# One instruction per row for the hidden layer, and the weighted sums in two bursts

## What is computed

```python
hi = jnp.einsum('bsh,hk->bsk', x, W1[:H])
hj = jnp.einsum('bsh,hk->bsk', x, W1[H:])
h = jax.nn.relu(hi[:, :, None, :] + hj[:, None, :, :] + b1)
y = jnp.einsum('bijk,kl->bijl', h, W2) + b2
y = _layernorm(y, gamma, beta)
out = jnp.einsum('bij,bijh->bih', adj, y)
```

## Time and profile before

| | |
|---|---|
| median of 3 runs | 2622.48 us |
| the profiled execution, first to last instruction | 2621.4 us |
| granted TensorE clock, mean | 0.998 |
| TensorE busy (weight loads) | 2577.0 us, 98% (2049.5 us, 78%) |
| VectorE busy | 2337.8 us, 89% |
| ScalarE busy | 2332.6 us, 89% |
| GpSimd busy | 1999.1 us, 76% |

### The profile page before, as it was taken

How to read it: one execution, slowest core, us unless ns; L and a number is a source line. 1 busy time by engine, 2 the same in 40 slices (tenths; PEclk the granted TensorE clock), 3 DMA queues, 4 the chain that set the end, 5 groups by cost and what they waited for, 6 DMA issues and landing times.

```text
span 2621.4 us, 77145 instructions
## 1 busy us (share of the span) xinstructions
PE 2577.0 (98%) x21263; PEld 2049.5 (78%) x21263; DVE 2337.8 (89%) x18135; ACT 2332.6 (89%) x3650; POOL 1999.1 (76%) x1163
## 2 busy tenths in 40 slices
PE   8999999999999999999999999999999999999997
PEld 7777777777777777777777777777777777777774
DVE  7889988989899889998898989988988999989897
ACT  7899899899998998989989889999899898998996
POOL 7777777777777777777777777777777777777773
PEclk9999999999999999999999999999999999999999
DMA  0000000000000000000000000000000000000000
GB/s 17 8 12 7 11 7 10 11 6 11 11 6 11 6 11 11 6 11 11 6 11 6 11 11 6 11 10 7 11 6 11 11 6 11 8 8 11 6 7 7
DMA packets 48051, 23.49 MB, mean 9 GB/s; under 512 B 6208, under 2 KB 47808, under 8 KB 47808
## 3 DMA queue, kind: packets, MB, share of 16 engines
q1 hardware_dynamic: 46512, 21.12, 2.9%
q10 hardware_dynamic: 1296, 0.20, 0.0%
HBM read 17.11 MB, written 4.19 MB: 8 GB/s over the span
## 4 chain that ended last, share of the span: by engine, by line
PE 58%; DVE 24%; issue 11%; ACT 6%; POOL 0%; ACTq 0%; DVEq 0%; DMA 0%
PE y_ps L529 42%; DVE squares L517 16%; PE agg_ps L573 12%; DVE q L517 3%; ACT y L263 3%; DVE x1e L488 2%; ACT h L281 1%; ACT L334 1%; PE prep_ps L529 1%; PE tail_ps L529 1%; DVE o_sb L455 1%; PE tail_ps L584 1%; PE att_ps L529 1%; DVE eT L509 0%; DVE si_cols L499 0%
## 5 line engine op out<-in xcount | busy, mean ns | idle before, releaser
L252 POOL TENSOR_TENSOR h<-bT,aT 128x1024 f32<-128x1024 f32 x1024 | 1951.1, 1919 | 584.3 <-PE y_ps L529 572.9
L529 PEld LDWEIGHTS y_ps<-w_pair,h 128*128 128x128 f32 x16384 | 1885.7, 192 | 313.0 <-DVE q L517 260.3
L529 PE MATMUL y_ps<-w_pair,h 128*128 128x128 f32 x16384 | 1991.3, 278 | 21.9 <-DVE q L517 9.3
L517 DVE CUSTOM_DVE_ANT_0 squares<-y_ps,y 128x128 bf16<-128x128 f32 x8192 | 1842.3, 282 | 185.0 <-ACT y L263 171.2
L263 ACT ACTIVATE y<-y_ps 128x508 f32<-128x508 f32 x2048 | 1162.4, 595 | 190.8 <-PE y_ps L529 173.9
L281 ACT ACTIVATE h<-h 128x1024 f32<-128x1024 f32 x1024 | 1085.3, 1060 | 10.2 <-POOL h L252 10.2
L517 DVE DVE_READ_ACCUMULATOR2_ANT q<- 128x1 f32 x8192 | 659.1, 80 | 0.0
L573 PE MATMUL agg_ps<-y,wz 128*32 128x512 f32 x4096 | 545.9, 606 | 1.7 <-DVE o_sb L455 1.7
L573 PEld LDWEIGHTS agg_ps<-y,wz 128*32 128x32 f32 x4096 | 81.1, 108 | 66.7 <-issue 3.1
L492 DVE CUSTOM_DVE_ANT_0 s_terms<-x1e,v1row 128x128 f32<-128x128 f32 x64 | 99.5, 1554 | 0.1
L334 ACT ACT_TABLE_LOAD x64 | 82.1, 1283 | 4.3 <-DVE sj L504 3.2
(11 more groups left out here) (90 smaller groups left out, 740.4 us busy)
## 6 DMA issues: line engine op xcount, KB each, us to landing
x_in<-in_x_dram SPq DMA_DIRECT2D x64, 64.0 KB, 1.8
adj_in<-in_adj_dram SPq DMA_DIRECT2D x64, 64.0 KB, 1.9
x_res<-in_x_dram SPq DMA_DIRECT2D x64, 64.0 KB, 1.8
adj_res<-in_adj_dram SPq DMA_DIRECT2D x64, 64.0 KB, 1.9
out_dram<-x_out SPq DMA_DIRECT2D x64, 64.0 KB, 1.6
w<-in_L_gnn_W_dram ACTq DMA_DIRECT2D x1, 64.0 KB, 2.4
w1a<-in_L_gnn_W_dram SPq DMA_DIRECT2D x1, 64.0 KB, 2.2
w1b<-in_L_gnn_W_dram SPq DMA_DIRECT2D x1, 64.0 KB, 2.3
```

What stands on the lines that cost most here:

```text
L252: nc.gpsimd.tensor_tensor(h[:, u % HRING].rearrange("k (r g) s -> k r g s", g=GROUPS), bT[:, p, :].unsqueeze(1).unsqueeze(1).broadcast_to( ...
L517: last = nc.vector.tensor_tensor_reduce(out=squares[:, k % YRING, n, :], in0=y_ps[k % YRING][:, n, :], in1=y[:, p, i, :], scale=1.0, scala ...
L529: return nc.tensor.matmul(dst, lhsT, rhs, start=start, stop=stop)
```

## The change

Four things change. Each row of `h` is made by one instruction that adds and applies the relu: 7 of the 8 rows of a unit by GpSimd (`tensor_scalar` with an add and a max, the node's column as a per-partition scalar), 1 by ScalarE (an activation with a bias). The relu in place goes away. The weighted sums stand in two bursts of four chunks, after the pairs of u = 7 and of u = 13 of the slot that follows the batch's own. Around them other work moves: GpSimd makes `wz` at u = 6 in place of 8; TensorE transposes `o_sb` at u = 5 (from 6), multiplies with `w_back` at u = 7 (from 8) and makes the next batch's products behind the pairs of u = 7 (from in front of u = 9); ScalarE's copies move one unit earlier; VectorE's `adj_sum` and `x_beta` move to u = 8, and `project` from u = 10 to u = 8.

```diff
-    WEIGHTS_UNIT = 4
-    POOL_WEIGHTS_UNIT = 8
-    CHUNK_STEP = UNITS // CHUNKS
-    EARLY_CHUNKS = (UNITS - WEIGHTS_UNIT) // CHUNK_STEP
+    POOL_ROWS = 7
+    POOL_WEIGHTS_UNIT = 6
+    BURST = {7: range(0, CHUNKS // 2), 13: range(CHUNKS // 2, CHUNKS)}
...
+        def row(u, n):
+            return n % GROUPS * GROUP + u * QPU + n // GROUPS
...
-                    nc.gpsimd.tensor_tensor(
-                        h[:, u % HRING].rearrange("k (r g) s -> k r g s", g=GROUPS),
-                        bT[:, p, :].unsqueeze(1).unsqueeze(1).broadcast_to(shape),
-                        a_now.unsqueeze(3).broadcast_to(shape), ALU.add).then_inc(u_ready, 1)
+                    pool.sem_inc(pool_passed, 1)
+                    for n in range(POOL_ROWS):
+                        i = row(u, n)
+                        last = nc.gpsimd.tensor_scalar(h[:, u % HRING, n, :], bT[:, p, :], aT[:, p, i:i + 1], 0.0, ALU.add, ALU.max)
+                    last.then_inc(h_pool, 1)
...
-            def relu(t, u):
-                act.wait_ge(u_ready, t * UNITS + u + 1)
-                nc.scalar.activation(h[:, u % HRING], h[:, u % HRING], ACT.Relu).then_inc(h_ready, 1)
+            def act_rows(t, p, u, first):
+                if u == 0:
+                    act.wait_ge(ab_sb_s, t + 1)
+                if not (first and u < HRING):
+                    act.wait_ge(y_in_psum, t * QUARTS + (u - HRING + 1) * QPU)
+                for n in range(POOL_ROWS, UNIT):
+                    i = row(u, n)
+                    last = nc.scalar.activation(h[:, u % HRING, n, :], bT[:, p, :], ACT.Relu, bias=aT[:, p, i:i + 1])
+                last.then_inc(h_act, 1)
...
-                    if tail and u == 7:
+                    if tail and u == 6:
                         act.wait_ge(oT_ps_s, t - 1)
...
-                    if prep and u == 8:
+                    if prep and u == 7:
                         prep_copies(t + 1, early + 1)
...
-                    if tail and (u, e) == (6, 0):
+                    if tail and (u, e) == (8, 0):
                         dve.wait_ge(xres_loaded[p], nth16(half, p, -2) * 2)
...
-                    if tail and (u, e) == (7, 0):
+                    if tail and (u, e) == (8, 1):
                         dve.wait_ge(adj_sum_ready, t - 1)
...
-                    if prep and (u, e) == (10, 0):
+                    if prep and (u, e) == (8, 0):
                         if early >= 1:
-                            dve.wait_ge(u_ready, t * UNITS)
+                            dve.wait_ge(h_pool, t * UNITS)
+                            dve.wait_ge(h_act, t * UNITS)
                         project(t + 1, 1 - p)
...
-                    if tail and u == 6:
+                    if tail and u == 5:
                         pe.wait_ge(o_stored, t - 1)
                         nc.tensor.transpose(tail_ps[:, 0, :], o_sb[:], ident[:]).then_inc(oT_ps_s, 1)
...
-                    if tail and u == 8:
+                    if tail and u == 7:
                         pe.wait_ge(oT_sb_s, t - 1)
                         mm(tail_ps[:, 1, :], oT_sb[:], w_back[:]).then_inc(f_ps_s, 1)
-                    if prep and u == 9:
-                        prep_products(t + 1)
...
-                        pe.wait_ge(h_ready, t * UNITS + u + 1)
+                        pe.wait_ge(h_pool, t * UNITS + u + 1)
+                        pe.wait_ge(h_act, t * UNITS + u + 1)
...
-                    if gather and chunk_due and chunk >= 0:
-                        if chunk == 0:
-                            pe.wait_ge(w_ready, t)
-                            if early >= 2:
-                                pe.wait_ge(o_stored, t - 1)
-                        weighted_sums(1 - p, chunk)
-                    if tail and chunk_due and chunk < 0:
-                        weighted_sums(p, chunk + CHUNKS)
+                    if prep and u == 7:
+                        prep_products(t + 1)
+                    if gather and u in BURST:
+                        for chunk in BURST[u]:
+                            if chunk == 0:
+                                pe.wait_ge(w_ready, t)
+                                if early >= 2:
+                                    pe.wait_ge(o_stored, t - 1)
+                            weighted_sums(1 - p, chunk)
```

More of the change, by code:

```diff
@@ L135, in gnn_pair_kernel @@
         ab_ps_s, ab_sb_s = sem("ab_in_psum"), sem("ab_in_sbuf")
-        u_ready, h_ready = sem("preact_ready"), sem("h_ready")
+        h_pool, h_act = sem("h_rows_from_pool"), sem("h_rows_from_act")
         y_in_psum, y_stored, q_done = sem("y_in_psum"), sem("y_stored"), sem("q_done")
@@ L145, in gnn_pair_kernel @@
             sem(n) for n in ("adj_sum_ready", "x_beta_ready", "sj_ready", "si_sum_ready", "si_ready"))
-        s_passed = sem("statistics_wait_passed")
+        s_passed, pool_passed = sem("statistics_wait_passed"), sem("pool_row_wait_passed")
         out_ready = sem("out_ready")
@@ L249, in slot @@
                         pool.wait_ge(y_in_psum, t * QUARTS + (u - HRING + 1) * QPU)
-                    shape = [K, QPU, GROUPS, S]
-                    a_now = aT[:, p, :].rearrange("k (g r) -> k r g", g=GROUPS)[:, u * QPU:(u + 1) * QPU, :]
-                    nc.gpsimd.tensor_tensor(
-                        h[:, u % HRING].rearrange("k (r g) s -> k r g s", g=GROUPS),
-                        bT[:, p, :].unsqueeze(1).unsqueeze(1).broadcast_to(shape),
-                        a_now.unsqueeze(3).broadcast_to(shape), ALU.add).then_inc(u_ready, 1)
+                    pool.sem_inc(pool_passed, 1)
[3 more added lines that the diff above has]
+                    last.then_inc(h_pool, 1)
             run_slots(pool, slot)
@@ L295, in _ @@
             for u in range(2):
-                relu(0, u)
+                act_rows(0, 0, u, True)
             def slot(t, half, p, pairs, prep, gather, tail, finish, early):
@@ L337, in slot @@
                         if ahead < UNITS:
-                            relu(t, ahead)
+                            act_rows(t, p, ahead, early == 0)
                         elif prep:
-                            relu(t + 1, ahead - UNITS)
+                            act_rows(t + 1, 1 - p, ahead - UNITS, False)
                         for k in range(u * QPU, (u + 1) * QPU):
                             if k == 0 and early >= 2:
-                                act.wait_ge(agg_done, (t - 2) * CHUNKS + EARLY_CHUNKS)
-                            if k == EARLY_CHUNKS * CHUNK and early >= 2:
                                 act.wait_ge(agg_done, (t - 1) * CHUNKS)
@@ L605, in slot @@
                             last.then_inc(y_in_psum, 1)
-                    chunk = (u + 1 - WEIGHTS_UNIT) // CHUNK_STEP - 1
-                    chunk_due = (u + 1 - WEIGHTS_UNIT) % CHUNK_STEP == 0
-                    if gather and chunk_due and chunk >= 0:
-                        if chunk == 0:
-                            pe.wait_ge(w_ready, t)
-                            if early >= 2:
-                                pe.wait_ge(o_stored, t - 1)
-                        weighted_sums(1 - p, chunk)
-                    if tail and chunk_due and chunk < 0:
-                        weighted_sums(p, chunk + CHUNKS)
+                    if prep and u == 7:
[7 more added lines that the diff above has]
+                            weighted_sums(1 - p, chunk)
             run_slots(pe, slot)
```

## The result

The changed kernel takes 5044.9 us (median of 4 runs) against 2622.5: 1.924 times as long, 95% interval 1.921 to 1.926. The profiled execution has a span of 5042.3 us. I had forecast 2626 us and a range of 2535 to 2720.

What follows compares the result with a forecast made beforehand. TensorE was taken to bound the kernel, VectorE close behind; TensorE's 2.0 and VectorE's 2.5 us are spent in idling, so 2621.4 + 7 - 3 = 2625.4 us profiled, 2626 us in the runs, range 2535 to 2720.

Steps and rivals of the forecast that it cites:

- the cover by TensorE's 1.79 us per unit: GpSimd's seven rows, 1.7 us per unit, stay hidden behind TensorE's 1.79 us; this ends at 0.35 us per row.
- Rival B: GpSimd becomes the bound: slower, 2950 us at 0.40 us per row, 2740 at 0.37; chance 0.13.
- VectorE's gain: VectorE's slow instructions wait less for the end of GpSimd's instruction: about 2.5 us per batch, bounds 0 and 2.9.
- the four operations I had named: VectorE's `x1e`, two `s_terms` and `eT`, together 4.15 us per batch by median, 1.26 at their shortest.
- The burst's price: Four weighted-sum chunks in a row on TensorE cost 3.77 us in place of 4.76, saving 1.0 per burst.
- the refill of 1.82 us: Behind a burst VectorE restarts only when a quart is made and copied, 1.82 us after the first pair load.
- the wait for sd: VectorE waits 0.85 us for ScalarE's root, which comes after a copy and a table load, at u = 2.
- the one for `o_sb`: TensorE, free at 13.7 us, waits at u = 5 for VectorE's `o_sb`, done at 15.0.
- TensorE's 2.0 us: Saving of two bursts per batch; TensorE's own work falls from 39.4 to 37.4 us.
- the batch's twelve small ones: TensorE's transposes, `w_back`, scores and preparation, 0.11 us each, 1.3 us per batch.
- Rival C: VectorE's blocked instructions stay blocked by GpSimd's gapless rows: 43 us per batch, 2790 us; chance 0.03.
- rival A: The refill is cheaper and TensorE stays the bound: faster, 2452 us, halfway 2540; chance 0.16.

Runs made afterwards that it cites:

- the run of the forms: A kernel with GpSimd only, twelve instruction forms 20 times each in a row; the changed kernel's row took 0.69 us from start to start.
- the halved adds: GpSimd's add of 1024 as two of 512: 2801.0 us in the kernel with bursts and moved steps (3130.3 undivided), 2610.0 us in the kernel before.
- the run with two rows: The changed kernel with 2 rows of a unit on GpSimd, 1 on ScalarE, five left as written once: 2647.4 us, ratio 1.0097.
- the run with pairs: The kernel before's schedule, weighted sums in pairs of chunks, 2 rows on GpSimd, 1 on ScalarE, five written once: 2526.8 us, ratio 0.964.
- the kernel with bursts only: The kernel before with the bursts and every moved step, h made as before (one add of 1024, relu on ScalarE): 3130.3 us, ratio 1.193.

## Why the prediction was wrong

**The step that failed** is the price of GpSimd's row: "so I take the affine select's 0.24 and keep 0.14 and 0.53". It measures 0.69 us from start to start, above even my upper bound. I had taken it from an instruction of another kind with the same 128 columns. With 112 rows the term is 77 us per batch, where I had 27, and so the cover by TensorE's 1.79 us per unit was gone. The rows of before could have given a higher bound: the product of 128 columns, 0.53, plus another pass for the max at an eighth of the add of 1024, 0.24, is an estimated 0.77. That bound would have held without being the mechanism: in the run of the forms the second operation is only 0.11 us, and one operation with a constant costs 0.53 already.

**Rival B** was the right mechanism: GpSimd as the bound, deciding from r = 0.35, a period of 112 r + 0.8. With r = 0.69 its formula gives 78 us, measured 77.7. Its price (0.37 to 0.40) and its chance (0.13) were too small, and the range left it out.

**VectorE's gain** came true for the four operations I had named: 2.6 us by the medians in the changed kernel against the 2.5 forecast. Of its whole work the gain was 0.8 us per batch there, and it is part of no time, since GpSimd bounds. That VectorE waits for the end of GpSimd's instruction is what the ends and the halved adds show. By the Trainium skill's rule (SBUF — State Buffer, who interferes with whom) the second one blocks for the whole instruction; the trace agrees, 1945 ns at an instruction of 1.9 us, 1079 at 1.04. But the forecast had the set of waiting operations fixed, and which of them wait depends on the schedule.

**The burst's price** (1.19 + 3 x 0.86), the refill of 1.82 us (first `squares` at 1018.57 behind the load at 1016.75), the wait for sd and the one for `o_sb` all stood in the run with two rows: 2647 against 2626. So as far as that run tells, with five rows left out, the change would have gained nothing with a cheap row either; TensorE's 2.0 us go to the refill and the waits. One of its sums is loose: "the batch's twelve small ones" holds the attention product, which is listed beside them. One batch of the run has 12 such loads in all, which gives the 39.4 us stated for TensorE's work; as listed it would be 39.6.

**ScalarE** fell to 27.9 us per batch (26 forecast), which is worth nothing in the changed kernel.

**Rival C** fell; **rival A** fell for this schedule, though the run with pairs shows where the saving can be had.

## What to carry to other kernels

When an instruction is absent from the trace, bound its price per element and its fixed part apart; a row of the same size from another kind of instruction is no bound. If the whole forecast hangs on that price, as here (0.24 assumed, 0.35 the limit), run the form alone first: twenty in a row settled it. Cutting a wide GpSimd instruction into narrow ones shortens what VectorE's operations wait for, but more of them meet one, and the fixed part is paid each time: here two pieces paid, four did not. Group work on TensorE only as far as the ring behind it holds work for the next engine.

## What the runs showed of the hardware that was not expected

- GpSimd's `tensor_scalar` with two operations costs 3.33 ns per column of 128 partitions, twice its `tensor_tensor` add (1.67 ns), though that reads two inputs, one of them broadcast.
- In the changed kernel the recorded length of such an instruction is 2.1 us by median, three times the distance of the starts (0.69); with GpSimd alone it is 0.71. `wz` lasts 1.9 us there in place of 0.53, and 0.46 to the next start. It grows in the course of the run: the first three `wz` last 0.61, 0.67 and 1.14 us. With the same seven rows and no bursts the mean stays at 712 ns, so the number of rows is not the cause; what is was not tried.
- A wide `tensor_scalar` of VectorE (`v`, `si_cols`), at 0.29 us nearly always before, took 1.5 to 1.8 us when it met GpSimd's long instruction.
- TensorE's granted clock falls behind its waits also in kernels where it is busy for most of the time: 0.955 on average in the kernel with bursts only (TensorE busy for 85%), against 0.998 before (98%).
